# Layer-norm statistics of the main half: short operations from VectorE and ScalarE to GpSimd, and the normalization in two ScalarE passes

## The reference

```python
xn = (x - mean(x)) / sqrt(var(x) + 1e-5)          # per position, over 1024
# recurrent branch; bitlinear: weights quantized to -1, 0, 1 times a row scale
r = sigmoid(bitlinear(xn, Wr)); kv = bitlinear(xn, Wk) * bitlinear(xn, Wv)
scale = exp(t * log(sigmoid(decay)))              # t = position
state = cumsum(kv / clip(scale, 1e-10)) * scale
s = bitlinear(rmsnorm(r * state, ln_w), Wo)
# expert branch: one of 8 experts for each position, by the largest gate score
g = silu(xn + expert_out[argmax(xn @ gate_w.T)])
out = x + s * g
```

## Time and profile before

| | us |
|---|---|
| median of 2 runs | 1285.14 (1268.17 and 1302.12) |
| profiled execution | 1270.03 |
| its span, slowest core (7) | 1268.2 |
| spans of the 8 cores | 1259.3 to 1268.2 |
| PE busy | 908.3 (72%) |
| DVE busy | 691.3 (55%) |
| ACT busy | 453.3 (36%) |
| POOL busy | 86.2 (7%) |

### The profile page before, as it was taken

One profiled execution on the slowest core, in us unless ns is written; L12 is line 12 of the kernel. 1 busy time (PEld: TensorE's weight loads), 2 busy tenths in 40 slices (PEclk: granted clock), 3 DMA queues, 4 the chain that ended last, 5 costly groups with the idle time before them and its releaser, 6 DMA issues.

```text
span 1268.2 us, 17398 instructions; the slowest of 8 cores (1259.3 to 1268.2 us)
## 1 busy us (share of the span) xinstructions
PE 908.3 (72%) x5760; PEld 552.1 (44%) x5760; DVE 691.3 (55%) x1381; ACT 453.3 (36%) x929; POOL 86.2 (7%) x220
## 2 busy tenths in 40 slices
PE   0222236666566658998999899898899799899764
PEld 0111124555444544553554454454455365365321
DVE  4777755565665335454564474473573573573443
ACT  4444443333333254404604604703702802802102
POOL 0000001111111100000000000000000000000000
PEclk9999997777777779999999899999899999999877
DMA  3333345788886874524553552562571571661760
GB/s 102 103 114 110 127 125 106 192 206 191 202 178 160 213 181 129 204 67 123 210 171 129 193 181 97 194 213 71 197 236 57 192 250 34 225 210 33 233 199 33
DMA packets 37672, 196.23 MB, mean 155 GB/s; under 512 B 5840, under 2 KB 7888, under 8 KB 30416
## 3 DMA queue, kind: packets, MB, share of 16 engines
q0 software_dynamic: 17280, 134.23, 35.6%
q1 hardware_dynamic: 20304, 60.91, 15.3%
HBM read 186.73 MB, written 25.17 MB: 167 GB/s over the span
## 4 chain that ended last, share of the span: by engine, by line
PE 57%; DVE 23%; DMA 6%; issue 6%; ACT 6%; DVEq 1%; SPq 0%; ACTq 0%; POOL 0%; POOLq 0%
PE pb L610 25%; PE pb L501 24%; DMA ebuf<-escr 5%; DVE qwb L271 5%; PE pb L664 5%; DVE sC L267 3%; DVE sC L555 2%; PE pb L277 2%; DVE wvT L292 2%; DVE wkT L292 2%; ACT xn_fm L414 2%; DVE sD L539 2%; DVE sD L549 2%; DVE woT L290 1%; DMA out<-s_sb 1%
## 5 line engine op out<-in xcount | busy, mean ns | idle before, releaser
L610 PE MATMUL pb<-ebuf,xn_fm 128*128 128x512 bf16 x2048 | 468.7, 390 | 55.2 <-DVE moe L626 29.4
L610 PEld LDWEIGHTS pb<-ebuf,xn_fm 128*128 128x128 bf16 x2048 | 203.2, 100 | 310.7 <-issue 89.1
L626 DVE SCALAR_TENSOR_TENSOR moe<-pb,ohb,moe 128x512 bf16<-128x512 f32 x224 | 167.9, 749 | 71.3 <-PE pb L610 55.2
L277 PE MATMUL pb<-identb,qwb 128*128 128x128 bf16 x384 | 48.6, 307 | 212.5 <-DVE qwb L271 212.5
L501 PE MATMUL pb<-xn_fm,wkT 128*128 128x256 bf16 x1024 | 134.4, 300 | 7.0 <-ACT xn_fm L414 7.0
L277 PEld LDWEIGHTS pb<-identb,qwb 128*128 128x128 bf16 x384 | 37.2, 139 | 223.7 <-issue 223.7
L501 PEld LDWEIGHTS pb<-xn_fm,wkT 128*128 128x128 bf16 x1024 | 109.0, 107 | 32.3 <-issue 8.9
L501 PE MATMUL pb<-xn_fm,wvT 128*128 128x256 bf16 x1024 | 114.4, 273 | 2.7 <-DVE sC L523 2.7
L501 PEld LDWEIGHTS pb<-xn_fm,wvT 128*128 128x128 bf16 x1024 | 100.1, 98 | 16.1 <-issue 3.0
L257 ACT ACTIVATE sA<-stageQ 128x1024 f32<-128x1024 f32 x48 | 50.7, 1057 | 98.7 <-DVE sC L267 96.5
L561 ACT COPY carryb<-sC 128x1 f32<-128x1 f32 x64 | 6.7, 188 | 213.5 <-DVE sC L555 213.5
(11 more groups left out here) (101 smaller groups left out, 838.4 us busy)
## 6 DMA issues: line engine op xcount, KB each, us to landing
ebuf<-escr POOLq DMA_DIRECT2D x48, 2048.0 KB, 9.8
ebuf<-ewt POOLq DMA_DIRECT2D x64, 256.0 KB, 14.4
escr<-ebuf POOLq DMA_DIRECT2D x8, 2048.0 KB, 7.6
stageQ<-wk SPq DMA_DIRECT2D x16, 512.0 KB, 3.2
stageQ<-wv SPq DMA_DIRECT2D x16, 512.0 KB, 3.3
xb<-xpre SPq DMA_DIRECT2D x16, 512.0 KB, 10.3
xb<-xmain SPq DMA_DIRECT2D x16, 512.0 KB, 13.0
stageQ<-xmain SPq DMA_DIRECT2D x16, 512.0 KB, 10.7
```

The costliest lines, as they stand in the source:

```text
L277: return [e.matmul(bank[:, i2 * 128:(i2 + 1) * 128], qwbf[:, (4 * q + i2) * 128:(4 * q + i2 + 1) * 128], ident[:], start=True, stop=True) ...
L610: ins.append(e.matmul(bank[:, 0:512], xnf[:, kc * ST + j * 128: kc * ST + (j + 1) * 128], kbuf[:, kc * D + nh * 512: kc * D + nh * 512 + 512],
L626: e.scalar_tensor_tensor(dst, bank[:, 0:512], ohcol, src2, ALU.mult, ALU.add)],
```

## The change

The prefix layer norm stays as it is; the diff only moves its operations into the `prefix` branch. In the main half (the `else` branch, executed for 8 tiles) these change:

- The mean is no longer formed on ACT. POOL forms the negative mean `nm` from the sum.
- The division of the squares by D goes to POOL and takes the 1e-5 with it (`s2g`).
- The square of the mean is one ACT operation (`m2c`), and the logarithm takes it with `s2g` as its bias. The two DVE operations for the variance go.
- The copy `acol2` goes from DVE to POOL, and `nbc` is no longer computed.
- The pass over x with scale and bias becomes two: ACT writes x - mean in f32 into `sA`, then ACT scales `sA` and writes `xn_tm`.

```diff
+                op("gpsimd", lambda e: [
+                    e.tensor_scalar(nm[:, 0:NSUB], t1c[:, 0:NSUB], -1.0 / D,
                                     None, ALU.mult)],
+                   reads=["t1c"], writes=["nm"])
+                op("scalar", lambda e, xs=xs: [
+                    e.activation(sA[:, j * D:(j + 1) * D], xs[:, j * D:(j + 1) * D],
+                                 AF.Square, accum_out=sq2[:, j:j + 1])
+                    for j in range(NSUB)],
+                    reads=[f"x{pp}"], writes=["sA", "sq2"])
+                op("gpsimd", lambda e: [
+                    e.tensor_scalar(s2g[:, 0:NSUB], sq2[:, 0:NSUB], 1.0 / D,
+                                    float(np.float32(1e-5)), ALU.mult, ALU.add)],
+                   reads=["sq2"], writes=["s2g"])
+                op("scalar", lambda e: [
+                    e.activation(m2c[:, j:j + 1], t1c[:, j:j + 1], AF.Square,
+                                 scale=1.0 / D)
+                    for j in range(NSUB)],
+                    reads=["t1c"], writes=["m2c"])
+                op("scalar", lambda e: [
+                    e.activation(lnc[:, j:j + 1], m2c[:, j:j + 1], AF.Ln,
+                                 bias=s2g[:, j:j + 1], scale=-1.0)
+                    for j in range(NSUB)],
+                    reads=["m2c", "s2g"], writes=["lncol"])
+                op("scalar", lambda e: [
+                    e.activation(acol[:, j:j + 1], lnc[:, j:j + 1], AF.Exp, scale=-0.5)
+                    for j in range(NSUB)],
+                    reads=["lncol"], writes=["acol"])
+                op("gpsimd", lambda e: [
+                    e.tensor_copy(acol2[:, 0:NSUB], acol[:, 0:NSUB])],
                    reads=["acol"], writes=["acol2"])
-                op("vector", lambda e: [
-                    e.scalar_tensor_tensor(nbc[:, 0:NSUB], mcol[:, 0:NSUB], -1.0,
-                                           acol[:, 0:NSUB], ALU.mult, ALU.mult)],
-                   reads=["mcol", "acol"], writes=["nbc"])
-                op("scalar", lambda e, xs=xs, xnt=xnt: [
-                    e.activation(xnt[:, j * D:(j + 1) * D], xs[:, j * D:(j + 1) * D],
-                                 AF.Identity, bias=nbc[:, j:j + 1],
-                                 scale=acol2[:, j:j + 1])
-                    for j in range(NSUB)],
-                    reads=[f"x{pp}", "nbc", "acol2"], writes=[f"xn_tm{pp}"])
+                op("scalar", lambda e, xs=xs: [
+                    e.activation(sA[:, j * D:(j + 1) * D], xs[:, j * D:(j + 1) * D],
+                                 AF.Identity, bias=nm[:, j:j + 1])
+                    for j in range(NSUB)],
+                    reads=[f"x{pp}", "nm"], writes=["sA"])
+                op("scalar", lambda e, xnt=xnt: [
+                    e.activation(xnt[:, j * D:(j + 1) * D], sA[:, j * D:(j + 1) * D],
+                                 AF.Identity, scale=acol2[:, j:j + 1])
+                    for j in range(NSUB)],
+                    reads=["sA", "acol2"], writes=[f"xn_tm{pp}"])
```

More of the change, by code:

```diff
@@ L189, in build_nc @@
         nbc = sb("nbc", [128, 2])
+        nm = sb("nm", [128, 2])
+        m2c = sb("m2c", [128, 2])
+        s2g = sb("s2g", [128, 2])
         rsv = sb("rsv", [128, 2])
@@ L336, in emit_ln_math @@
                     reads=[f"x{pp}"], writes=["t1c"])
-            else:
+                op("scalar", lambda e: [
+                    e.mul(mcol[:, j:j + 1], t1c[:, j:j + 1], 1.0 / D)
+                    for j in range(NSUB)],
+                    reads=["t1c"], writes=["mcol"])
                 op("scalar", lambda e, xs=xs: [
                     e.activation(sA[:, j * D:(j + 1) * D], xs[:, j * D:(j + 1) * D],
-                                 AF.Identity, accum_out=t1c[:, j:j + 1])
+                                 AF.Square, accum_out=sq2[:, j:j + 1])
@@ new lines, in emit_ln_math @@
+                op("scalar", lambda e: [
+                    e.mul(s2c[:, j:j + 1], sq2[:, j:j + 1], 1.0 / D)
+                    for j in range(NSUB)],
+                    reads=["sq2"], writes=["s2c"])
+                op("vector", lambda e: [
+                    e.scalar_tensor_tensor(nvar[:, j:j + 1], mcol[:, j:j + 1],
+                                           mcol[:, j:j + 1], s2c[:, j:j + 1],
+                                           ALU.mult, ALU.subtract)
+                    for j in range(NSUB)],
+                    reads=["mcol", "s2c"], writes=["nvar"])
@@ new lines, in emit_ln_math @@
+                op("scalar", lambda e: [
+                    e.activation(lnc[:, j:j + 1], nvar[:, j:j + 1], AF.Ln,
+                                 bias=cst[:, 0:1], scale=-1.0)
+                    for j in range(NSUB)],
+                    reads=["nvar", "cst"], writes=["lncol"])
+                op("scalar", lambda e: [
+                    e.activation(acol[:, j:j + 1], lnc[:, j:j + 1], AF.Exp, scale=-0.5)
+                    for j in range(NSUB)],
+                    reads=["lncol"], writes=["acol"])
@@ new lines, in emit_ln_math @@
+                op("gpsimd", lambda e: [
+                    e.tensor_scalar(nm[:, 0:NSUB], t1c[:, 0:NSUB], -1.0 / D,
+                                    None, ALU.mult)],
+                   reads=["t1c"], writes=["nm"])
+                op("scalar", lambda e, xs=xs: [
+                    e.activation(sA[:, j * D:(j + 1) * D], xs[:, j * D:(j + 1) * D],
+                                 AF.Square, accum_out=sq2[:, j:j + 1])
+                    for j in range(NSUB)],
+                    reads=[f"x{pp}"], writes=["sA", "sq2"])
@@ new lines, in emit_ln_math @@
+                op("gpsimd", lambda e: [
+                    e.tensor_copy(acol2[:, 0:NSUB], acol[:, 0:NSUB])],
+                   reads=["acol"], writes=["acol2"])
+                op("scalar", lambda e, xs=xs: [
+                    e.activation(sA[:, j * D:(j + 1) * D], xs[:, j * D:(j + 1) * D],
+                                 AF.Identity, bias=nm[:, j:j + 1])
+                    for j in range(NSUB)],
+                    reads=[f"x{pp}", "nm"], writes=["sA"])
+                op("scalar", lambda e, xnt=xnt: [
+                    e.activation(xnt[:, j * D:(j + 1) * D], sA[:, j * D:(j + 1) * D],
+                                 AF.Identity, scale=acol2[:, j:j + 1])
+                    for j in range(NSUB)],
+                    reads=["sA", "acol2"], writes=[f"xn_tm{pp}"])
```

14 lines of the change are left out of this document (2 added, 12 removed).

## The result

| | before | changed |
|---|---|---|
| median, us | 1268.57 (10 runs) | 1319.77 (11 runs) |
| ratio | | 1.0413, 95% interval 1.0386 to 1.0439 |
| span of the slowest core, profiled | 1268.2 (core 7) | 1322.3 (core 5) |
| mean granted clock over the 8 cores | 0.907 to 0.920 | 0.889 to 0.897 |

The changed kernel is 4.1% slower, on all eight cores (spans 1308.9 to 1322.3 us). With the 10 runs of the kernel before, its median is 1268.57 and no longer the 1285.14 of the first two. The ratio leaves out the executions in which the cores of one die ran at a lower clock (1302.12 before, 1337.72 and 1350.36 changed). Lines of the changed kernel's code are shifted: the norm's passes are 376, 385, 411 and 416, POOL's operations 381, 390 and 408, the scan preparation 539 (DVE) and 544 (ACT), the transposes 435, the casts 441, the experts 637, the store 315.

The account below looks back on a forecast made before the run. PE waits for ACT's chain from norm to casts, and at the first norm for POOL's held queue. Profiled span 1268.2 + loop 24.3 + first norm 18.4 + clock 9.4 + 1.8 around it = 1322 us (1307 to 1332).

Parts of the forecast that it names:

- What bounds: Main loop: ACT's chain from the next tile's norm to the casts sets expert 3's start; loop loss 24.3 us.
- The hold on POOL: First main-half norm: POOL's new operations stand behind the store L312, which waits for the expert's loads, delaying the first cast.
- the first norm's term: First cast at 472.9 instead of 452.50, 20.4 us; less 2 us for the later load of x: 18.4 (15.4 to 20.4).
- The wait for sA: Each loop pass: DVE's filling of sA waits for the second pass, delaying ACT's exponential and casts; 3.7 us a pass altogether.
- The price of the passes: Norm's pass over x: two pairs with one column operand, 2.15 us each (2.0 to 2.37), 0.1 before each; xn_tm 1.2 later.
- The statistics: Norm's mean and variance: POOL's s2g replaces ACT and DVE steps; table load 0.59 after the squares' end, 0.5 us earlier altogether.
- The clock: Experts 3 and 4: longer PE idling gives all seven passes a 2.3 us dip, 16.1 less 6.7: 9.4 us, up to 13.6.
- Rival 3: Loop: clock dips at expert 2 and experts 3 and 4 every pass, 34 us instead of 9.4, total 1347; chance 0.07.
- The total: Whole kernel: 1322 us, 4.1% more, between 1307 and 1332; the forecast was given 0.75.

Follow-up runs that it names:

- the moved store: Changed kernel with the last prepared expert's store issued on POOL behind the first layer norm's three operations instead of ahead: 1303.39 us, ratio 1.0293.
- the buffer edit: Changed kernel with the centred tile parked in sD instead of sA, still two passes: 1296.46 us, ratio 1.0235.
- two-pass kernel: Kernel before with only the normalization in two passes through sA; statistics and copies stay on ACT and DVE, none on POOL: 1314.19 us, ratio 1.0370.
- filled kernel: Changed kernel with 14 useless products on PE between the second and third group of transposes in the loop's seven passes: 1308.38 us, ratio 1.0334.

## Why the prediction was right, step by step

- **What bounds.** ACT's chain from the norm to the casts sets expert 3's start: shown from both sides. Lengthening it by what the change adds moved expert 3 by 24.2 us in seven passes (24.3 foretold; 25.3 in the mean of the eight cores); taking the exponential out of it made ACT wait for PE and the kernel faster.
- **The hold on POOL.** Right in mechanism: 13.6 us by the moved store, and a single copy behind it costs 11.4 at the first cast. The size of the first norm's term, 18.4, was 1.4 over the measured 17.0: the load of x did move behind the norm (465.32), and the store came 17.3 us after the norm's start in place of 20.6. I had allowed 2 us of 5 for this; it was 3.3, between two different cores. Left out was PE's clock behind this norm: nothing on the slowest core, 1.6 us in the mean and up to 3 on others.
- **The wait for sA.** DVE's L539 waits for the second pass, ACT idles 2.39 us ahead of the exponential: both as foretold, and 2.5 us a pass by the buffer edit. The gate and the evictions behind L539 cost nothing more.
- **The price of the passes.** A pair with one column operand took 2.17 to 2.19 us, where I had 2.15 between 2.0 and 2.37. The Trainium skill's 93 ns for each column operand (ScalarE: Activation LUTs, What ACT_TABLE_LOAD costs) gave an estimated 2.17; by that rule, the trace agrees. The 0.1 between the pairs was a little small: it is 0.15 in two norms, 0.26 in five and 0.54 in one (the row at 933.91), although POOL's copy is long done by then. The kernel with the copy on DVE has 0.15 in all eight. What ACT waits for was not settled; it is at most 0.4 us a norm.
- **The statistics.** From the squares' end to the table load 0.48 us with POOL (0.78 in one pass), 0.59 foretold. The gain is real (0.2 to 0.5 us a norm in the loop). The two-pass kernel without it is slower than the one with the store moved (1.0370 against 1.0293), by more than the 4 us that this makes at most, since PE loses more to its clock there; with one pass over x the gain is not seen (0.9989).
- **The clock.** 8.2 us against 9.4 on the slowest cores, 6.3 in the mean of eight. All seven passes now have a dip, of 1.3 to 2.8 us (15.29 to 16.82 us for the pair, 13.97 without one); the filled kernel shows that it comes from the idle stretch. I had put all passes at the 2.3 us of one, and the kernel before loses more on most of its cores than the 6.7 us that I took off. That the term came out near its size is partly luck: the two-pass kernel shows that nearly the same stretch can cost three times as much.
- **Rival 3** did not come true, though the slowest core looks as if it had by half. There expert 2 ran slow in all seven passes (8.5 to 9.3 us in place of 7.07), behind waits of 3.8 to 4.4 us, mostly for its weights; in the kernel before it did so in four of seven. Over the eight cores it was slow in 21 of 56 passes, and in 20 before, so these traces don't show that the change has a part in it. It cost nothing, because PE waits for the casts in any case and has the time.
- **Not foretold:** 2.0 us in one pass, where a late expert ran at the lower clock after 2.20 us of idle time (785.09). Two passes of the filled kernel and one of the kernel with the store moved show such a loss at about the same size; over the eight cores the rest of the passes took 0.4 to 6.8 us more than the 361.3 of an undisturbed loop. It was not followed up.
- **The total.** 1322 against 1319.8 (1323.9 for the profiled execution) is in part luck. The first norm was 1.4 us and the clock 1.2 us under what was foretold, and two things that were not foretold made up for them: the late expert's 2.0 us, and the 2.2 us ahead of the first norm, which is no more than the cores differ among themselves.

## What to carry to other kernels

A small operation is as late as the slowest wait in front of it on its engine's queue. Before moving one to an idle engine, look in the timeline for what that engine stands waiting for at that moment, in each stage and not on average: POOL was 7% busy here and cost 13.6 us. A scratch buffer used once more adds a wait for everyone who writes it next, and the price is found in what stands behind that writer. And where an engine idles ahead of a bound engine's work, ask first which operation in its order isn't needed yet: placing the scan preparation behind the casts won 0.8% (0.9921), where all small operations on POOL, with the queue out of the way, won nothing that can be told (0.9989).

## What was not expected of the hardware

PE's loss of clock after an idle stretch is not a function of the stretch's length alone in these traces. Two kernels with 8.0 and 8.7 us of idle ahead of the first transposes, and the same order of work after it, lost 1.3 and 4.2 us in the two projections that follow (8.47 + 7.15 and 9.79 + 8.67 us, where 7.15 is the undisturbed one), on every core. The changed kernel idled 20.0 to 22.4 us there and lost 1.4 to 4.5 us in the three projections that follow, depending on the core. In its loop core 5 idled 32.6 us ahead of expert 3 over the seven passes and core 1 55.3, and experts 3 and 4 took 112.0 us on both. Means over eight cores are steadier: 19.1, 25.4, 31.7 and 49.8 us of this idle time went with 104.0, 105.5, 107.6 and 111.8 us (the kernels with the exponential later, before, with sD, and changed), though the two-pass kernel has 114.9 at 49.3. An estimate of such a term from one row or one core is good to a factor of two or so.
